# Token rows, threshold search and slot chain placed inside the shared network of a one-core audio-tower kernel

## The reference, cut to what matters

```
xn      = layernorm(h)                                   # 6016 x 256
scores  = softmax(xn @ gate_w.T).T                       # 16 experts x 6016 tokens
topk_weight, topk_idx = top_k(scores, 752)               # each expert takes 752 tokens
shared  = (gelu(xn @ Sg.T) * (xn @ Su.T)) @ Sd.T         # hidden width 512
expert e: (gelu(xg @ Wg.T) * (xg @ Wu.T)) @ Wd.T * topk_weight, added at topk_idx   # hidden width 1024
out     = h + shared + sum over experts
```

## Time and profile before

| | |
|---|---|
| median of 3 runs | 2146.38 us (2142.93 to 2149.76) |
| profiled execution | 2143.69 us |
| its span, first to last instruction | 2141.9 us |
| PE, DVE, ACT, POOL busy | 1763.1, 1230.0, 908.1, 943.2 us |
| mean granted TensorE clock | 0.913 of full |

### The profile page before, as it was taken

How to read it: one execution, slowest core, us unless ns; L and a number is a source line. 1 busy time by engine, 2 the same in 40 slices (tenths; PEclk the granted TensorE clock), 3 DMA queues, 4 the chain that set the end, 5 groups by cost and what they waited for, 6 DMA issues and landing times.

```text
span 2141.9 us, 48763 instructions
## 1 busy us (share of the span) xinstructions
PE 1763.1 (82%) x15898; PEld 1280.2 (60%) x15898; DVE 1230.0 (57%) x3696; ACT 908.1 (42%) x1862; POOL 943.2 (44%) x921
## 2 busy tenths in 40 slices
PE   6957899999999845439999238999999999999997
PEld 5844566666666524327777235666666666666665
DVE  3875788888888843315555664444444444444442
ACT  3534556666666531113332144444444444444442
POOL 3851344444444320002222014666666666666666
PEclk9987999999999975559999558999999999999999
DMA  5614555555555511110000023333333333333312
GB/s 167 205 33 88 119 127 131 126 129 129 129 127 129 115 51 39 46 45 22 29 29 29 15 82 131 88 90 89 88 88 88 88 88 88 88 88 88 88 27 29
DMA packets 211857, 186.32 MB, mean 87 GB/s; under 512 B 157136, under 2 KB 192464, under 8 KB 205648
## 3 DMA queue, kind: packets, MB, share of 16 engines
q1 hardware_dynamic: 184912, 141.12, 24.8%
q0 software_dynamic: 26880, 44.36, 9.6%
HBM read 134.51 MB, written 50.44 MB: 86 GB/s over the span
## 4 chain that ended last, share of the span: by engine, by line
issue 33%; PE 20%; POOL 18%; DMA 12%; DVE 10%; SPq 3%; ACT 1%; POOLq 1%; DVEq 1%; PEld 0%; ACTq 0%; PEldq 0%
POOL arena L573 7%; DMA score_table<-arena 4%; DMA out<-hidden,arena 4%; POOL arena L599 4%; PE psum L1520 3%; POOL out L608 3%; DVE arena L981 3%; DVE psum L989 2%; PE psum L1360 2%; PE psum L1303 2%; PE psum L1257 2%; SPq L416 2%; PE psum L1325 2%; PE psum L1271 2%; PE psum L1537 1%
## 5 line engine op out<-in xcount | busy, mean ns | idle before, releaser
L573 POOL TENSOR_TENSOR arena<-arena 128x376 f16<-128x376 f32 x320 | 348.5, 1179 | 580.2 <-ACT arena L644 563.9
L1520 PE MATMUL psum<-arena,hidden 128*128 128x376 f16 x3072 | 503.2, 323 | 42.4 <-DVE arena L1192 41.5
L1520 PEld LDWEIGHTS psum<-arena,hidden 128*128 128x128 f16 x3072 | 296.5, 98 | 244.9 <-DVE arena L1192 62.8
L644 ACT ACTIVATE arena<-arena 128x376 f16<-128x376 f32 (+5 forms) x610 | 287.5, 474 | 59.4 <-DVE arena L1192 53.6
L1192 DVE SCALAR_TENSOR_TENSOR arena<-psum,arena 128x376 f32<-128x376 f32 x256 | 140.1, 547 | 281.3 <-ACT arena L821 186.9
L821 ACT ACTIVATE arena<-psum 128x376 f32<-128x376 f32 x256 | 123.7, 483 | 401.4 <-PE psum L1520 395.6
L981 DVE CUSTOM_DVE_ANT_0 arena<-psum,constants 128x188 f32<-128x188 f32 x768 | 227.9, 345 | 108.4 <-PE psum L1257 107.3
L644 ACT ACTIVATE arena<-psum 128x188 f32<-128x188 f32 (+8 forms) x467 | 173.8, 400 | 259.8 <-PE psum L1409 46.4
L1537 PE MATMUL psum<-hidden,arena 128*128 128x256 f16 (+1 forms) x2304 | 256.7, 273 | 15.3 <-POOL arena L573 15.3
L1537 PEld LDWEIGHTS psum<-hidden,arena 128*128 128x128 f16 (+1 forms) x2304 | 229.0, 103 | 39.8 <-POOL arena L573 18.4
L693 ACT ACTIVATE arena<-psum 128x564 f32<-128x564 f32 x256 | 164.0, 641 | 103.8 <-PE psum L1271 102.2
(11 more groups left out here) (153 smaller groups left out, 2798.6 us busy)
## 6 DMA issues: line engine op xcount, KB each, us to landing
arena<-q_halves SPq DMA_DIRECT2D x384, 47.0 KB, 2.5
arena<-k_halves SPq DMA_DIRECT2D x384, 47.0 KB, 2.2
arena<-e_g SPq DMA_DIRECT2D x16, 1024.0 KB, 5.0
arena<-e_u SPq DMA_DIRECT2D x16, 1024.0 KB, 5.4
arena<-e_d SPq DMA_DIRECT2D x16, 1024.0 KB, 5.1
arena<-x_t SPq DMA_DIRECT2D x32, 376.0 KB, 3.5
weighed<-arena POOLq DMA_DIRECT2D x32, 376.0 KB, 4.0
token_table<-arena SPq DMA_DIRECT2D x8, 799.0 KB
```

Source lines behind the costliest of these rows:

```text
L573: nc.gpsimd.tensor_tensor(dst, f, hi, ALU.subtract).then_inc(ready, 1)
L644: return nc.scalar.activation(dst, src, ACT.Copy, scale=scale)
L1520: last = mm(bank[2 * (s % 2) + i][:, 0:CHUNK], w_, a, start=n == 0, stop=n == 5)
```

## The change

Stages 1, 2 and 3 become one, written out without loops as 64 steps (`STEPS`; 16 chunks x 4), with no barrier between them and none ahead of the one-hot stage or the experts.

- **Rows.** DVE (even batches) and POOL (odd batches) normalise two batches per step through a ring of four buffers XR of 94 x 512. SP writes each batch's rows at once (`rows_out`, 94 partitions x 2 x 1024 B), and a buffer is filled again when its rows have been turned and its transfer has landed (`row_out`). Steps 0 to 14 turn two batches each, between the gate and up products.
- **Scores.** The gate products are now made turned, 96 products of 32 x 376 per group of 4 chunks (`turned_logits`), turned back (`logits_back`), and the softmax is taken once for each of 4 groups. The 16 scores of a row go to `token_table` in a transfer of their own, 94 partitions x 16 x 64 B (`scores_out`), and the turned scores as two transfers of 128 partitions x 376 B (`turned_scores_out`).
- **Search.** 30 rounds (before: 32), one per step in steps 24 to 53. SC8 is loaded when all score transfers have landed; DVE waits for it at step 23.
- **Slot chain.** The same operations, spread over steps 53 to 60.
- **Down products.** 48 at m = 1 for chunks 0 to 4, then 12 per step, five steps late.
- **Experts.** SP loads expert 0's weights after the last down product and the landing of `out`, into a place that the one-hot matrices don't use; POOL clears 32 partitions x 272 of each XG rather than all of it, and starts when `IDX` is listed.

The diff, cut to its core:

```diff
+STEPS = 4 * KS
+PREP = 15
+WHOLE = 5
+QUADS = 4
+FIRST = 23
+ROUNDS = 30
...
+        def normal_rows(eng, tensor_scalar, b):
+
+            if b >= RING:
+                eng.wait_ge(rt_done, b - RING + 1)
+                eng.wait_ge(row_out[b % RING], 16 * (b // RING))
+            for qt in range(2):
+                t = 2 * b + qt
+                last = tensor_scalar(XR[b % RING][0:HT, qt * D:(qt + 1) * D], H[0:HT, t, :], MV[0:HT, t, 0:1],
+                                     RSTD[0:HT, t, :], ALU.subtract, ALU.mult)
+            last.then_inc(row_ready[b % 2], 1)
...
-            def group(g, par):
-                sp.wait_ge(score_ready, g + 1)
-                hold(sp)
-                sp.dma_start(xtab[bass.ts(g, 2 * GROUP * HT), :].rearrange("(t p) n -> p t n", p=HT), ROWS3[par][0:HT, :, :]).then_inc(table_out[par], 16)
-                sp.wait_ge(sct_ready, g + 1)
-                hold(sp)
-                sp.dma_start(sctab[:, bass.ts(g, 2 * GROUP * HT)], SCT[par][0:E, :]).then_inc(table_out[par], 16)
...
+            def rows_out(b):
+                sp.wait_ge(row_ready[b % 2], b // 2 + 1)
+                sp.dma_start(xtab[b * S:(b + 1) * S, 0:D].rearrange("(t p) n -> p t n", p=HT),
+                             XR[b % RING][0:HT, :].rearrange("p (t n) -> p t n", t=2)).then_inc(row_out[b % RING], 16)
+
+            def scores_out(q):
+                sp.wait_ge(score_ready, q + 1)
+                sp.dma_start(xtab[q * 16 * HT:(q + 1) * 16 * HT, D:ROW].rearrange("(t p) n -> p t n", p=HT),
+                             PSC[0:HT, q * 16 * E:(q + 1) * 16 * E].rearrange("p (t n) -> p t n", n=E)).then_inc(score_out, 16)
+
+            def turned_scores_out(q):
+                sp.wait_ge(sct_ready, q + 1)
+                for h in range(2):
+                    sp.dma_start(sctab[:, (2 * q + h) * CH:(2 * q + h + 1) * CH].rearrange("e (t n) -> t e n", n=HT),
+                                 SCT[q % 2][:, h * HT:(h + 1) * HT]).then_inc(sct_out[q % 2], 16)
+
+            def chunk_out(k):
+                sp.wait_ge(sh_added, 2 * k + 2)
+                sp.dma_start(out[k * CHUNK:(k + 1) * CHUNK, :].rearrange("(t p) n -> p t n", p=HT),
+                             SOUT[k % 2][0:HT, :].rearrange("p (t n) -> p t n", t=4)).then_inc(sh_out[k % 2], 16)
+
+            for b in range(RING):
+                rows_out(b)
+            for s in range(STEPS):
+                k, m = divmod(s, 4)
+                if RING + 2 * s < B:
+                    rows_out(RING + 2 * s)
+                    rows_out(RING + 2 * s + 1)
+                if m == 2 and 1 <= k <= QUADS:
+                    scores_out(k - 1)
+                if m == 0 and 2 <= k <= QUADS + 1:
+                    turned_scores_out(k - 2)
+                if s == 4 * QUADS + 4:
+                    for par in range(2):
+                        sp.wait_ge(sct_out[par], 32 * QUADS // 2)
+                    sp.dma_start(SC8, sctab[:, :].rearrange("e (c n) -> (e c) n", c=8)).then_inc(sc8_in, 16)
+                if m == 3 and 1 <= k <= WHOLE:
+                    chunk_out(k - 1)
+                if m == 2 and k >= WHOLE + 2:
+                    chunk_out(k - 2)
+            for k in range(KS - 2, KS):
+                chunk_out(k)
             def load(e, i):
                 src = (e_g, e_u, e_d)[i]
                 sp.dma_start(WST[:, i * 2048:(i + 1) * 2048], src[e, :, :]).then_inc(w_in[i], 16)
 
-            for i in range(3):
-                load(0, i)
+            sp.wait_ge(down_done, STEPS)
+            load(0, 0)
+            for par in range(2):
+                sp.wait_ge(sh_out[par], 16 * (KS // 2))
+            load(0, 1)
+            load(0, 2)
...
+            pool.wait_ge(rstd2_done, 1)
+            normal_rows(pool, nc.gpsimd.tensor_scalar, 1)
+            normal_rows(pool, nc.gpsimd.tensor_scalar, 3)
+            for s in range(STEPS):
+                k, m = divmod(s, 4)
+                if RING + 2 * s < B:
+                    normal_rows(pool, nc.gpsimd.tensor_scalar, RING + 2 * s + 1)
+                c = slice(m * CHUNK, (m + 1) * CHUNK)
+                low_hidden(SHL[k % 2][:, c], SHF[m], SHH[k % 2][:, c], hh_ready, s + 1, hl_ready)
...
+            pool.wait_ge(idx_listed, 16)
             for par in range(2):
-                nc.gpsimd.memset(XG[par], 0.0).then_inc(xg_set, 1)
+                nc.gpsimd.memset(XG[par][96:128, (SLOT_TILES - 1) * ROW:], 0.0).then_inc(xg_set, 1)
+            for par in range(2):
+                pool.wait_ge(sh_out[par], 16 * (KS // 2))
...
+            def count(r):
+                if r == 0:
+                    dve.wait_ge(sc8_in, 16)
+                find.link(nc.vector.tensor_tensor(CAND, THR, BITI[:, r:r + 1], ALU.bitwise_or))
                 nc.vector.tensor_scalar(HIT, SC8, CAND.bitcast(F32), None, ALU.is_ge, ALU.add, accum_out=COUNT).then_inc(count_ready, 1)
...
+            normal_rows(dve, nc.vector.tensor_scalar, 0)
+            normal_rows(dve, nc.vector.tensor_scalar, 2)
+            low_rows(0)
+            low_rows(1)
+            done = FIRST + ROUNDS
+            for s in range(STEPS):
+                k, m = divmod(s, 4)
+                dve.wait_ge(gel_ready, s + 1)
+                if s >= RING:
+                    dve.wait_ge(hl_ready, s - RING + 1)
+                nc.vector.scalar_tensor_tensor(SHF[m], bank[2 * (s % 2) + 1][:, 0:CHUNK], HSCALE / WSCALE, SGEL[s % 2],
+                                               ALU.mult, ALU.mult).then_inc(hf_ready, 1)
+                if s < PREP:
+                    low_rows(2 * s + 2)
+                if RING + 2 * s < B:
+                    normal_rows(dve, nc.vector.tensor_scalar, RING + 2 * s)
+                if s < PREP:
+                    low_rows(2 * s + 3)
+                if FIRST < s <= done:
+                    decide(s - FIRST - 1)
+                if FIRST <= s < done:
+                    count(s - FIRST)
+                if m == 2 and 1 <= k <= WHOLE:
+                    down_out(k - 1, 0)
+                    down_out(k - 1, 1)
+                if m == 3 and k > WHOLE:
+                    down_out(k - 1, 0)
+                if m == 1 and k > WHOLE + 1:
+                    down_out(k - 2, 1)
+                if m == 0 and 1 <= k <= QUADS:
+                    logits_less_max(k - 1)
+                if m == 1 and 1 <= k <= QUADS:
+                    scores_of(k - 1)
...
+            def down(n_):
+                k, i, u = n_ // 4, n_ // 2 % 2, n_ % 2
+                if i + u == 0:
+                    pe.wait_ge(hl_ready, 4 * k + 4)
+                if u == 0 and k >= 1:
+                    pe.wait_ge(sh_added, 2 * k + i - 1)
...
+            def turned_logits(q):
+                pe.wait_ge(rtl_ready, 8 * q + 8)
+                if q >= 1:
+                    pe.wait_ge(sh_added, 2 * q - 1)
+                n = 0
+                for c in range(2):
+                    w = slice(W_GATE + c * E, W_GATE + c * E + 32)
+                    for low_w, low_x in ((False, False), (True, False), (False, True)):
+                        for g in range(4):
+                            last = mm(bank[4][32 * g:32 * g + 32, 0:CHUNK], (WL if low_w else WH)[:, w],
+                                      (TOKL if low_x else TOKH)[:, 4 * q + g, c, :], start=n == 0, stop=n == 5)
+                        n += 1
...
+            turn_rows(0)
+            turn_rows(1)
+            done = FIRST + ROUNDS
+            for s in range(STEPS):
+                k, m = divmod(s, 4)
+                if m == 0:
+                    pe.wait_ge(rtl_ready, 2 * k + 2)
+                if s >= 2:
+                    pe.wait_ge(hf_ready, s - 1)
+                gate_up(k, m)
+                if s < PREP:
+                    turn_rows(2 * s + 2)
+                    turn_rows(2 * s + 3)
+                if m == 0 and 1 <= k <= QUADS:
+                    logits_back(k - 1)
+                if m == 3 and 1 <= k <= QUADS:
+                    turn_scores(k - 1)
+                if m == 3 and k < QUADS:
+                    turned_logits(k)
+                if m == 1 and 1 <= k <= WHOLE:
+                    for i in range(4):
+                        down(4 * k - 4 + i)
+                if s >= 4 * WHOLE + 5:
+                    down(s - 5)
+                if FIRST < s <= done:
+                    pe.wait_ge(count_ready, s - FIRST)
+                    mm(bank[7][:, 0:1], C[:, C_ONES:C_ONES + 128], COUNT, start=True, stop=True).then_inc(total_done, 1)
+                if s == done + 2:
```

More of the change, by code:

```diff
@@ L192, in build @@
[L192 to L203, removed]
+        TOKH, TOKL = (at3(2 * T, F16).rearrange("p (k c n) -> p k c n", k=KS, c=2) for _ in range(2))
@@ new lines, in build @@
+        prep = at3.at
+        XR = [at3(2 * D) for _ in range(RING)]
+        PSC = at3(TILES * E)
+        LT = at3(CHUNK)
+        SCT = [at3(2 * HT) for _ in range(2)]
+        LMAX, LSUM, LINV = at3(E), at3(E), at3(E)
+        SD2 = at3(TILES)
```

(55 more changed lines are left out.)

374 lines of the change are left out of this document (191 added, 183 removed).

## The result

The changed kernel takes 2091.36 us (median of 4, 2089.13 to 2093.56) against 2144.65 for the kernel before in the same job (a set of kernels measured together): ratio 0.9749, 95% interval 0.9726 to 0.9772. The forecast was 2097.

The account below looks back on a forecast made before the run. It took a two-engine DMA queue to bound the kernel up to the SC8 load, then PE. Span 2141.9 less 44 (one-hot stage starting earlier) and 4 (experts' start) gave 2094, forecast as 2097 us; own range 2051 to 2132, wider 2050 to 2155.

Parts of the forecast that it names:

- The queue on two engines bounds everything up to SC8: Before the SC8 load: transfers from 94 partitions share two DMA engines in order, 216 us; DVE's first count at about 1020.
- Rows at 48 GB/s, 128.3 us: In the queue before SC8: 32 row transfers, 6.16 MB at 48 GB/s, 4.0 us each, 128.3 us in all.
- my 4 us for gaps: In the queue before SC8: gaps between transfers, nothing to 0.4 us each for 36 of them, taken as 4 us (0 to 15).
- Scores at 16 ns a packet, 48 us: In the queue before SC8: four score transfers of 1504 64 B packets, 16 ns each by a line through two rows, 48 us.
- the second rival: Score transfers: 64 B packets are dear, so the change ends slower; 2169 us at 40 ns, 2223 at 57.8; chance 0.13.
- Cover counted at nothing: Up to SC8, the queue hides POOL's normalisation (0.7 to 2.4 us for two instructions), row turns, ACT table loads and turned logits.
- After the count, 149 us with PE full: From DVE's first count at 1020 to the one-hot stage at 1169: PE sets the pace, 144.8 us plus start and end.
- The term for the 30 rounds: PE's work after the first count: each search round costs 0.4 us beyond the products, 12.2 us for 30.
- The one-hot stage untouched: The one-hot stage, 59.6 us, was given no change in the sum; the early expert weights hide in it.
- Start of the experts, 4 us: From slot list to first expert product, 25.4 us before: smaller clearing, no barrier, earlier weights gain 4 us (2.5 to 8).
- The sum: Whole kernel: span 2141.9 less 44 before the one-hot stage and 4 at the experts' start, 2094; 2097 us as measured time.
- First rival: Merged stage: rows go over other engines, the queue does not hold and PE sets all of it; 1993 us, chance 0.09.

Follow-up runs that it names:

- experiment 1: Changed kernel with only its row transfers sent in pieces of 80 and 14 partitions instead of 94: 1992.3 us, ratio 0.929 to the kernel before.
- experiment 2: Changed kernel with rows, scores and output chunks all sent in pieces of 80 and 14 partitions: 1969.17 us, ratio 0.9185 to the kernel before.
- experiment 3: Changed kernel with its row transfers sent in two pieces of 47 partitions: 2229.84 us, ratio 1.0395 to the kernel before.
- experiment 5: Changed kernel with each score transfer sent a second time, into a DRAM table nobody reads: 2120.52 us, ratio 0.9882 to the kernel before.
- experiment 7: Changed kernel without the high-by-low product in gate and up from step 25 on, 8 instead of 12 products a step: 2067.42 us.
- experiment 6: Changed kernel with the old start of the experts (barrier, XG cleared whole, expert 0's weights after the barrier): 2090.24 us.
- experiment 8: Changed kernel with all transfers in pieces of 80 and 14, in one job with old and new start of the experts: 1972.98 and 1971.0 us.

## Why the prediction was right, point by point

- **The queue on two engines bounds everything up to SC8.** Shown by experiments 1 to 3 and 5. First normalisation to first count: forecast 221.8 us (798.2 to 1020), measured 218.9. Steps 14 to 23 did not run as free as I had it: the outputs queue behind the rows too, and DVE stood 7.8 us for the landing of one, until 999.7. SC8 came later still, so it cost nothing.
- **Rows at 48 GB/s, 128.3 us.** Too cheap. In steady flow 43 packets a microsecond leave (344 in 8 us, experiment 3), 4.4 us a row, 141 us in all; with my 4 us for gaps I was 9 short. The rate of 48 GB/s came from 2 us within an `out` transfer, twice as long as a row transfer; no run changes the length alone.
- **Scores at 16 ns a packet, 48 us.** Too dear: 11.8 ns, 35 us, 13 over. That the errors of these two terms cancelled to 4 us was luck. My line went through prices worked out from the DMA share, and the share adds up the times of packets that overlap: worked out in the same way, 23.7% of 16 engines for 170 packets, a 64 B packet has 22 ns, while the queue moves on by one in 11.8. For the 1024 B packet the two are close, 50.6 (13.6%, 344 in 8 us) and 46.5 ns. What counts in a sum is the rate. The rule on 512 B that stood beside the second rival (the Trainium skill, DMA: Bandwidth & Descriptors, Specifications) would have made them dearer: a packet priced as one of 512 B would be 23 ns, half of the 46.5 (an estimate). The 11.8 ns do not bear that out; whether some part of them is such a cost, no run shows.
- **Cover counted at nothing.** POOL's normalisation is 1.22 us an instruction, at the upper end of what I gave it; hidden at 8.9 us per step. In experiment 2, where the cover is gone, PE still sets the pace.
- **After the count, 149 us with PE full.** Measured 141.9 (1021.4 to 1163.3), PE full as forecast but for the first 4.1 us at half clock, and experiment 7 shows that the time is PE's. The term for the 30 rounds was too big: the whole stretch leaves some 0.2 us for each rather than 0.4.
- **The one-hot stage untouched.** Not quite: 62.0 us against 59.6. Two of its four groups of products took 6.6 and 6.5 us instead of 5.8 and 5.6; these are the quarters whose matrices now lie both in the arena, and the last of them ends the stage 0.9 us later. DVE waited 1.8 us for PE's first group instead of 0.5, with 1.5 us of PE's issue inside that group. Neither was tested.
- **Start of the experts, 4 us.** The two traces are 5.1 apart, which fits, but not for my reasons alone: with the old start put back, 2.5 of them return in the trace of experiment 6 and none in its median, and the pair of experiment 8 has 2.0 by the medians and 1.2 by the traces. So the edits of the start are worth 1 to 2 us, and the term was too big.
- **The sum.** From first normalisation to one-hot stage 53.8 us less (414.6 to 360.8), start of the experts 5.1 less, one-hot stage 2.4 and the experts' loop 2.0 more, and the attention before it all ended 4.3 later, which the other traces of this case scatter by as well (first normalisation from 795.2 to 802.5): 50.2 by the spans, 53.3 by the medians, 49 forecast. The closeness of 50 and 49 is in part luck again: the merged stage gave 10 us more than the 44 of the sum, and 8.7 us that I had put at nothing took most of it back. The recorded sum is also added up 1.5 us short: 2094 with 1.8 and 2.7 is 2098.5, not 2097.
- **First rival.** It is what experiment 2 makes real, and its 1993 us was 22 to 24 too many: I had 267 us for the merged stage, PE needed 245. A good third of the difference is a count that I had wrong from the start, in the section on the change as well: the turned logits are 24 products per group of 4 chunks and 96 in all, not 96 per group. In experiment 2, from the first normalisation to the first count:

```profile
L1506 PE MATMUL psum<-arena,weights_hi 128*32 128x376 f16 x64 | 4.6, 325 | 0.0
L1506 PE MATMUL psum<-arena,weights_lo 128*32 128x376 f16 x32 | 2.7, 322 | 0.0
```

  That is at most 7.3 us of PE in place of 15.

## What to carry to other kernels

A DMA share that stood still near two sixteenths while other work waited was here the sign of transfers with a bad partition count; look at that before moving any stage. Cutting 94 partitions into 80 and 14 gained more in the old kernel than the whole rebuilding did, and made the rebuilding worth twice as much, since the row stage could be hidden behind PE's work only once its queue was no longer the longer of the two. The transfers from 94 partitions shared their two engines in order, so their times were to be summed along the queue, up to the one that somebody waited for; and the price to sum is the rate at which packets leave, not the DMA share.

## What the hardware showed that I had not expected

In the changed kernel a 64 B packet, written 1088 B apart, cost 11.8 ns on each of two engines, a quarter of the 46.5 ns of a 1024 B one. The same tensor_scalar over 94 x 256 numbers took 0.40 us on DVE and 1.22 us on POOL there.
